# Reordering the weight-square passes, two raw loads and the first attention steps in a two-layer transformer block

## The reference, cut to what matters

```
x = x + fake_quant(layernorm(x)) @ fake_quant(ctx)                 # 2 x 512 x 1024
h = layernorm(x);  x = x + h @ W.T + b + 2 * routed_lora(h)
q = rope(layernorm(x) @ wq);  k = rope(ctx @ wk);  v = ctx @ wv    # 32 heads of q, 8 of k and v
x = x + softmax(q k^T / sqrt(128) + mask) @ v @ wo
x = x + layernorm(x) @ W_up.T + top1_lora(layernorm(x))
```

## Time and profile before

| | |
|---|---|
| median of three runs | 1969.56 us (1968.51 to 1969.95) |
| the profiled execution | 1968.51 us, of which 1966.7 us are its span |
| mean granted clock of TensorE | 0.997 of full speed |
| PE busy | 98% of the span |
| DVE, ACT, POOL busy | 82%, 57%, 63% |

### The profile page before, as it was taken

How to read it: one execution, slowest core, us unless ns; L and a number is a source line. 1 busy time by engine, 2 the same in 40 slices (tenths; PEclk the granted TensorE clock), 3 DMA queues, 4 the chain that set the end, 5 groups by cost and what they waited for, 6 DMA issues and landing times.

```text
span 1966.7 us, 25859 instructions
## 1 busy us (share of the span) xinstructions
PE 1923.4 (98%) x8946; PEld 1008.1 (51%) x8950; DVE 1607.5 (82%) x2686; ACT 1126.1 (57%) x1795; POOL 1229.8 (63%) x753
## 2 busy tenths in 40 slices
PE   8999999989979999999999999999999999999999
PEld 6886787845434444444444444444444444444444
DVE  5887788688488988999888889888989999888663
ACT  5563555456366656666656566565566666666710
POOL 1542354333278777878778787777688787886700
PEclk9999999999999999999999999999999999999999
DMA  7663588669989987999978799899778988797822
GB/s 258 212 214 130 172 260 254 201 203 276 233 180 208 190 172 149 185 191 188 195 149 185 162 202 209 192 215 210 163 163 171 184 176 186 152 206 145 190 54 75
DMA packets 724433, 366.97 MB, mean 187 GB/s; under 512 B 627440, under 2 KB 650352, under 8 KB 724304
## 3 DMA queue, kind: packets, MB, share of 16 engines
q1 hardware_dynamic: 724304, 365.33, 79.4%
HBM read 182.79 MB, written 27.26 MB: 107 GB/s over the span
## 4 chain that ended last, share of the span: by engine, by line
PE 68%; DVE 3%; ACT 1%; DMA 1%; POOL 1%; issue 1%; SPq 1%; ACTq 0%; DVEq 0%
PE ps L43 23%; PE ps L44 22%; PE ps L45 22%; DVE psb L1824 1%; DVE pp L1839 1%; DMA x_lo<-x_scratch 1%; SPq L774 0%; POOL ua L2449 0%; DVE ta L1338 0%; ACT scan L2113 0%; ACT pp L2272 0%; DMA pT<-pp 0%; DVE x_lo L1853 0%; PE ps L1270 0%; ACT psb L2265 0%
## 5 line engine op out<-in xcount | busy, mean ns | idle before, releaser
L1839 DVE SCALAR_TENSOR_TENSOR pp<-psb,st,pp 128x1024 f16<-128x1024 f32 x256 | 398.1, 1555 | 30.4 <-ACT pp L2272 28.3
L2272 ACT ACTIVATE pp<-psb,st 128x1024 f16<-128x1024 f32 x256 | 293.4, 1146 | 201.4 <-DVE st L1834 192.1
L1824 DVE CUSTOM_DVE_ANT_0 psb<-ps,mask,sc 128x1024 f32<-128x1024 f32 x256 | 327.2, 1278 | 84.1 <-PE ps L45 83.2
L2265 ACT ACTIVATE psb<-psb,st 128x1024 f32<-128x1024 f32 x256 | 293.6, 1147 | 87.4 <-DVE st L1824 87.0
L2436 POOL TENSOR_SCALAR araw<-araw,kst 128x512 f32<-128x512 f32 x128 | 274.6, 2146 | 28.9 <-DMA araw<-in_wq 28.9
L2436 POOL TENSOR_SCALAR araw<-araw,sc 128x512 f32<-128x512 f32 x128 | 235.1, 1837 | 17.9 <-DMA araw<-in_wo 17.9
L2441 POOL TENSOR_TENSOR wol<-araw,woh 128x512 f16<-128x512 f32 x128 | 151.6, 1185 | 98.6 <-ACT woh L2207 98.6
L1853 DVE SCALAR_TENSOR_TENSOR x_lo<-ps,sc,x_lo 128x512 f32<-128x512 f32 x256 | 191.5, 748 | 17.3 <-PE ps L45 9.4
L43 PE MATMUL ps<-pT,vsb 128*128 128x512 f16 x512 | 194.1, 379 | 5.4 <-DMA pT<-pp 5.2
L43 PE MATMUL ps<-ksb,qsb 128*128 128x512 f16 x512 | 194.1, 379 | 4.7 <-DVE st L1824 3.3
L43 PE MATMUL ps<-woh,osb 128*128 128x512 f16 x512 | 194.1, 379 | 3.8 <-DVE x_lo L1853 3.7
(11 more groups left out here) (337 smaller groups left out, 3794.8 us busy)
## 6 DMA issues: line engine op xcount, KB each, us to landing
araw<-in_wq SPq DMA_DIRECT2D x128, 256.0 KB, 3.6
araw<-in_wo SPq DMA_DIRECT2D x128, 256.0 KB, 3.4
scan<-in_wq SPq DMA_DIRECT2D x64, 256.0 KB, 4.8
scan<-in_wo SPq DMA_DIRECT2D x64, 256.0 KB, 5.1
raw<-in_wv SPq DMA_DIRECT2D x16, 512.0 KB, 4.9
raw<-in_ctxT SPq DMA_DIRECT2D x16, 512.0 KB, 4.3
raw<-in_wk SPq DMA_DIRECT2D x16, 512.0 KB, 5.5
raw<-in_ctx SPq DMA_DIRECT2D x16, 512.0 KB, 4.6
```

The costliest lines, as they stand in the source:

```text
L1824: e.tensor_tensor_reduce(out=psb[:, n % 3, :], in0=pair(n % 2 * 2), in1=mask[:, i, :], scale=sc[:, 23 - H // 32:24 - H // 32], scalar=-LOW ...
L1839: e.scalar_tensor_tensor(out=pp[:, r, 1024:2048], in0=psb[:, r, :], scalar=st[:, n // 4 % 4, 16 + i:17 + i], in1=pp[:, r, 0:1024], op0=ALU ...
L2265: e.activation(P, P, ACT.Exp, bias=c[:, i:i + 1], scale=-1.0, accum_out=c[:, 8 + i:9 + i]).then_inc(a_exp.sem, 1)
L2272: e.activation(pp[:, r, 0:1024], psb[:, r, :], ACT.Copy, scale=st[:, n // 4 % 4, 16 + i:17 + i]).then_inc(a_ph.sem, 1)
```

## The change

It moves work, and adds and removes none.

- ACT, keys and values: the squares of a step are done at the end of that step. Before, they were done in the next step, behind its `split_hi`. Only for even steps does this change the order.
- SP: the raw loads of c19 and c21 move from step 59 (ahead of `turn_f(2)`) to the start of step 60 (behind it).
- ACT and SP, FFN stage: the 64 squares of `wo` are shared out in another way. Ten fewer come at the beginning, two fewer ahead of `h_hi(3)`, and 17 (before: 7) behind `lora_hi(1)`, thirteen of them ahead of `split_w(("q", 3))`. Ten loads of squares come behind `load_k(0)` and the masks 0 and 1, and the stores of x2, the raw loads of q4 and q5, `cosq` and `sinq` come behind these.
- PE: `square_sums("v")` moves from behind `q_part(1, ...)` to ahead of `q_part(0, ...)`.
- DVE: `output_sums` and `output_scales` come ahead of `q_end(1)`, and `scale_mask(0, 1)` ahead of `scores_max(0)`.
- ACT and POOL: `up_hi(1)` and its low part move from `(p, w)` = (61, 2) to (61, 3). On POOL the up tile now stands ahead of `q_lo` within a `w`, but no tile shares a `w` with a `q_lo` any more.

```diff
-UP_AT = {(59, 3): 0, (61, 2): 1, (62, 0): 2, ...
+UP_AT = {(59, 3): 0, (61, 3): 1, (62, 0): 2, ...
...
@@ sync_program, steps
             if s == 59:
                 e.wait_ge(a_kq.sem, a_kq.last)
                 load_raw("c20")
+            if s == 60:
+                load_raw("c19")
+                load_raw("c21")
...
                 if SQUARE_LOAD_STEP[m] in group:
                     load_square(m)
-            if s == 59:
-                load_raw("c19")
-                load_raw("c21")
             if s in FFN_LOW_AT and s < 63:
                 turn_f(FFN_LOW_AT[s])
...
@@ sync_program, behind the steps
-        load_squares(0, 14)
+        load_squares(0, 7)
         e.wait_ge(t_kv.sem, t_kv[63])
         weights_split(e)
         for n in range(4):
             load_w(("q", n))
-        load_squares(14, 21)
+        load_squares(7, 11)
         turn_f(4)
...
         turn_h(1)
-        load_squares(55, 57)
+        load_squares(45, 47)
         turn_h(2)
-        load_squares(57, 64)
+        load_squares(47, 54)
         turn_h(3)
-        for i in (4, 5):
-            store_x2(i)
         for o in range(2):
             e.wait_ge(d_khl[o].sem, d_khl[o][62 + o])
             e.wait_ge(d_vhl[o].sem, d_vhl[o].last)
         load_k(0)
         load_mask(0, 0)
+        load_mask(0, 1)
+        load_squares(54, 64)
+        for i in (4, 5):
+            store_x2(i)
+        for n in range(4, 6):
+            load_w(("q", n))
         for i in (4, 5):
             e.wait_ge(d_x[i].sem, d_x[i]["store"])
         e.dma_start(cosq[:, :], A["cosq"]).then_inc(d_tab.sem, 16)
         e.dma_start(sinq[:, :], A["sinq"]).then_inc(d_tab.sem, 16)
-        for n in range(4, 6):
-            load_w(("q", n))
-        load_mask(0, 1)
         load_mask(0, 2)
...
@@ tensor_program
         ffn_end(7)
+        square_sums("v")
...
         for w in range(4):
             q_part(1, w)
-        square_sums("v")
...
@@ vector_program
         q_end(0)
+        output_sums()
         scale_mask(0, 0)
+        output_scales()
         q_end(1)
-        output_sums()
+        scale_mask(0, 1)
         scores_max(0)
-        scale_mask(0, 1)
         row_scale(0)
         scores_max(1)
         p_lo(0)
-        output_scales()
         row_scale(1)
...
@@ scalar_program, steps
-            step_squares(steps_done)
-            steps_done = group
             if s in A_TURN_AT:
...
             if s in FFN_NORM_AT:
                 root(("f", FFN_NORM_AT[s]))
-        step_squares(steps_done)
+            for n in range(99):
+                if SQUARE_STEPS[n] in group:
+                    square(n)
...
         split_hi("w33")
-        output_squares(0, 14)
+        output_squares(0, 4)
         root(("f", 5))
...
         split_w(("q", 2))
-        output_squares(53, 57)
+        output_squares(43, 45)
         h_hi(3)
+        output_squares(45, 47)
         router_exp(1)
         lora_hi(1)
+        output_squares(47, 60)
         split_w(("q", 3))
-        output_squares(57, 64)
+        output_squares(60, 64)
         split_w(("q", 4))
...
```

More of the change, by code:

```diff
@@ L119 @@
 LAST_AT = {249: 0, 251: 1, 252: 2, 253: 3, 255: 4}
-UP_AT = {(59, 3): 0, (61, 2): 1, (62, 0): 2, (62, 1): 3, (62, 3): 4, (63, 0): 5, (63, 2): 6, (63, 3): 7}
+UP_AT = {(59, 3): 0, (61, 3): 1, (62, 0): 2, (62, 1): 3, (62, 3): 4, (63, 0): 5, (63, 2): 6, (63, 3): 7}
 UP_LOAD_AT = {(58, 0): 0, (58, 1): 1, (58, 2): 2, (60, 3): 3, (61, 0): 4, (62, 0): 5, (62, 2): 6, (62, 3): 7}
@@ L824, in sync_program @@
             load_w(("q", n))
-        load_squares(14, 21)
+        load_squares(7, 11)
         turn_f(4)
-        load_squares(21, 27)
+        load_squares(11, 17)
         turn_f(5)
-        load_squares(27, 36)
+        load_squares(17, 26)
         turn_f(6)
-        load_squares(36, 45)
+        load_squares(26, 35)
         turn_f(7)
-        load_squares(45, 50)
+        load_squares(35, 40)
         e.wait_ge(v_kr.sem, v_kr[63])
         turn_h(0)
-        load_squares(50, 55)
+        load_squares(40, 45)
         turn_h(1)
-        load_squares(55, 57)
+        load_squares(45, 47)
         turn_h(2)
-        load_squares(57, 64)
+        load_squares(47, 54)
         turn_h(3)
-        for i in (4, 5):
-            store_x2(i)
         for o in range(2):
@@ L2128, in scalar_program @@
         key_square(0)
[L2130 to L2135, removed]
         for group in steps():
@@ L2220, in scalar_program @@
         ffn_hi(5)
-        output_squares(14, 20)
+        output_squares(4, 10)
         root(("f", 6))
-        output_squares(20, 24)
+        output_squares(10, 14)
         ffn_hi(6)
-        output_squares(24, 29)
+        output_squares(14, 19)
         root(("f", 7))
         root(("h", 0))
-        output_squares(29, 34)
+        output_squares(19, 24)
         ffn_hi(7)
-        output_squares(34, 38)
+        output_squares(24, 28)
         root(("h", 1))
         h_hi(0)
-        output_squares(38, 43)
+        output_squares(28, 33)
         split_w(("q", 0))
@@ L2236, in scalar_program @@
         h_hi(1)
-        output_squares(43, 48)
+        output_squares(33, 38)
         split_w(("q", 1))
@@ L2240, in scalar_program @@
         h_hi(2)
[L2241 removed]
+        output_squares(38, 43)
         split_w(("q", 2))
[L2243 removed]
+        output_squares(43, 45)
         h_hi(3)
+        output_squares(45, 47)
         router_exp(1)
         lora_hi(1)
+        output_squares(47, 60)
         split_w(("q", 3))
[L2248 removed]
+        output_squares(60, 64)
         split_w(("q", 4))
@@ L2467, in gpsimd_program @@
                     split_w(next(splits))
-                if p < 62 and w == 2:
-                    q_lo(p + 2)
                 if (p, w) in UP_AT:
@@ L2473, in gpsimd_program @@
                     e.tensor_tensor(up(k, 1), raw3(k), up(k, 0), ALU.subtract).then_inc(p_up.sem, 1)
+                if p < 62 and w == 2:
+                    q_lo(p + 2)
             if p == 63:
```

## The result

The changed kernel takes 1981.96 us (median, 1980.71 to 1984.65), against 1969.76 us for the kernel before. The ratio is 1.0066, with a 95% interval of 1.0052 to 1.0081: 10 to 16 us slower. The forecast was 1980.2 us, slower.

The account below looks back on a forecast made before the run. PE, busy 98% of the span, bounds the kernel, so only its waits count: 2.5 + 5.4 + 1.9 - 0.6 + 2.1 = 11.3 us on 1968.5, with part of the median's offset 1980.2 us; range 1974 to 1986.

Parts of the forecast that it names:

- The four places named: PE's waits for `ctab`, before first FFN product, for last square and for `wo_add` at `t` = 249, forecast to grow.
- Step squares: Step 51: squares ahead of `split_hi` delay ACT's high part 1.86 us, so PE waits longer for `ctab`: +2.5 us.
- swallowed term of w31: Step 59: w31's low part comes 1.86 us later; PE's wait at step 62 is swallowed by the FFN-start wait.
- c19 and c21: FFN start: c19, issued behind `turn_f(2)`, lands late and delays DVE's chain, so PE's FFN starts 5.4 us later.
- `ts_sb` and the clock behind it: FFN stage: `h_hi(3)` earlier, PE's wait shrinks from 2.04 to 0.7 us, no halved clock behind: some 3 us gained.
- The last square: Before `q_part(0)`: PE waits for late-loaded squares, losing the `ts_sb` gain; +1.9 us on the old clock, bounds -3 and +6.
- DVE's order: First scores: wait of 1.30 us of `scores(1)` goes, `scores_max(0)` about 1 us later: -0.6 us, bounds -2 and +1.
- `up_hi(1)`: At `t` = 247 its activations delay `o_hi(60)`, and through DVE PE's `wo_add`: +2.1 us, bounds 0 and 3.
- c19 in time: Rival: c19 lands fast or DVE has other work, so 5.4 us shrinks to 1.9: 1976.7 us, chance 0.15.
- Hidden: Rival: PE's waits move about and the sum stays within 0.2%: 1970 us, chance 0.07.
- faster: Rival: gains at the attention start decide, delays at steps 51 and 59 don't reach PE: about -6, 1963 us, chance 0.08.
- The loads back up: Rival, attention start: last square at 531 us, `cosq` and q4 late, clock halved: 6 us over forecast, 1986 us, chance 0.10.

Follow-up runs that it names:

- the eight others: Eight other kernels that also leave the squares around step 51 where the kernel before has them; PE waits 2.4 to 3.5 us for `ctab` there.
- the FFN stage alone: Kernel before with new FFN-stage shares and order of squares and loads, `square_sums("v")` ahead of `q_part(0)`, DVE's old order: 1974.18 us, ratio 1.0024.
- `h_hi(3)` first: Kernel before with ACT doing squares 53 to 56 behind `lora_hi(1)`, not ahead of `h_hi(3)`, loads unmoved: 1967.55 us, ratio 0.9982.

## Why the prediction was right, point by point

- **PE is the bound, and each edit costs what it does to PE's waits**: right, but for the clock, which it had left to the range: 3.4 to 9.8 us of the loss are PE busy for longer. The four places named hold the four waits that grew in both profiles. Two waits were sized too small, for `ts_sb` (under 1 us forecast, 1.3 and 1.8 measured) and for the last square (3 to 5 us forecast, 5.8 and 6.2 measured).
- **Step squares**, forecast +2.5 us, swallowed term of w31 apart. Measured +3.5 alone and 3.1 to 3.9 in company. The place and the chain were right, and so was the delay of 1.86 us (DVE's wait at step 51 grew by 1.83 us over its usual 2.78). But the term was a sum of three: the stretch 319 to 407 us lost 5.0 us, where kernels without the edit lost 0 to 3.1; the stretch before it lost 1.3 to 2.4 us, most of it PE's wait for POOL's sum into `ctab` ahead of step 51 (1.4 and 1.8 us), which I had not followed; and step 24 won about 1.3 us on `a1T`, which I had not looked at. The row of 1.21 us for `ctab` was a lucky one: against the 2.9 us that the eight others have on average, the wait itself grew by about 1.9 us and not by 3.6.
- **c19 and c21**, forecast +5.4. Measured 2.6 to 3.0 us at the start of the FFN, +3.9 alone. The mechanism was right: issue behind the transpose, landing 5.4 to 5.8 us later (forecast 4.9), all of it in DVE's chain. Two things made the term too large. The transpose took 1.72 us and not 3.19, most likely because the loads that had run beside it were the very ones that moved (it took 1.79 us in the kernel with c19 alone). And the share of w31 was not there: PE's start of the FFN lost 2.6 to 3.0 us with the step squares moved, and 2.6 without; with the step squares alone PE waited 2.96 us there, as before. PE was late itself by then, since step 51, which would explain it; no run shows that apart.
- **Low part of c19 without POOL beside it**, forecast 1.34 us: 1.28, against 2.23 with POOL beside it. The Trainium skill (SBUF — State Buffer, Who interferes with whom) has the two engines lock each other out of a shared port pair; the trace agrees.
- **`ts_sb` and the clock behind it**, forecast a gain of 3. Measured 3.2 us in the kernel with the FFN stage alone, 1.9 to 2.3 in the changed one. The two squares put ahead of `router_exp(1)` took back part: the first of them waited 1.00 us for its load, and both lay in the chain. Taken alone and without these two, the same idea gave the 3.5 us of `h_hi(3)` first.
- **The last square**, forecast +1.9 net of that gain; this is the term that was mis-sized. The working from SP's issue of `load_k(0)` to the last square gave 15.2 us and the trace 15.0 (524.76 to 539.72), though the 1 us to the semaphore in it stands in no row. What failed stands ahead of it and behind it: SP came to `load_k(0)` at 524.76, 12.9 us behind its place in the kernel before, where the start of the FFN was only 10.9 later; the matmul on the path (1.0 us) and the halved clock behind the wait (1.2 us), which I had left out, came on top. Counted from the FFN's start, `q_part(0)` began 4.9 us late, where I had 1.9, and was 6.2 us late when the clock was up again, just over my upper bound of 6. What made SP 2 us late stays open.
- **DVE's order**, forecast -0.6. Alone 0.0 (-2.5 to +2.0 us), in the changed kernel 4.3 us by the ratios. I had costed it without asking when PE delivers the sums. That its worth hangs on the early matmul is likely (DVE's wait of 3.44 us for the sums is there only with the late one) but not shown: with both, and the loads where they were, the kernel was no faster than with the late matmul.
- **`up_hi(1)`**, forecast +2.1: the wait is 2.43 us, against 0.35, and the kernel with that edit alone is 2.8 us slower, sometimes with a halved clock behind.
- **The rivals.** "c19 in time" fell: the load landed 5.4 to 5.8 us behind its issue and not sooner than the 4.9 I had put. "Hidden" and "faster" fell with steps 51 and 59. "The loads back up" was nearer to the truth than its 0.10: its mechanism is there (6.19 us of waiting, a halved clock, q4 late behind it), and the c19 term, too high by 2.5 us, made room for it in the sum. So the total was right to 2 us partly by luck, because two errors cancelled: c19 too dear by 2.5, the last square too cheap by 3.

## What to carry to other kernels

A load that is moved takes its own traffic along: cost the transfers that it used to run beside as well as its own delay. A ring of buffers turns a late batch of loads into a blocked queue, and what stands behind it is late too; moving the consumer only changes which of the waits is seen. Before a term is sized from a wait of one microsecond in one trace, see whether that wait is the same in a second one.

## What was unexpected

- The same program had spans of 1986.7 and 1980.5 us in two profiles. The longer one ran at 1.2 GHz in more stretches, among them one at 215 us (granted clock 0.66), one at 1305 us and one at 1843 us (0.70 and 0.56 in the rows above); at 1.7 us each they would make 5 of the 6.2 us. Each stands behind a wait of PE, of 1.98, 2.05 and 2.43 us. The second profile has the last of these waits too, at 215 us one of 1.17, and at the place of 1305 us none over 0.6. Why the wait for `wo_add` at that place is 2.05 us in one execution and gone in the next, no run shows; the kernel with all but DVE's order had it at 1.90 us, with the clock at 1.00 behind it.
- A wait of one length did not always bring the lower clock: behind 2.43 us at `t` = 249 it was 0.56 in one profile and 1.00 in the other, of the same program. Behind waits of 4.8 us or more after the start it fell every time. Which of the two comes adds or saves 1.7 us per wait.
